# Sorted expert rows packed to 256 columns, scattered without router weights, and weighted by VectorE after a plain gather

## The chip, the core and the metric

The kernel runs on one core of a Trainium2 chip. Its engines are TensorE (PE, matrix products), VectorE (DVE), ScalarE (ACT), GpSimd (POOL) and SyncE (SP), each with its own queue of instructions, in order; 16 DMA engines move data between HBM and the on-chip memory. Engines wait for each other by semaphores. The metric is the device time of one execution in microseconds; lower is better.

## The reference

Everything is float32. The input x has 4 batches of 512 tokens and 256 columns, 16 tiles of 128 tokens in all.

```python
def ffn(x):                          # E = 16 experts, F = 96, top K = 2
    probs = softmax(x @ router_w)
    w, idx = top_k(probs, 2);  w = w / sum(w)
    h = silu(x @ gate_w[e]) * (x @ up_w[e])
    return sum over the token's two experts of w * (h @ down_w[e])

def attention(x):                    # 16 heads of 128, 4 key/value heads, rotary, causal
    ...

x = x + 0.5 * ffn(layernorm(x))
x = x + attention(layernorm(x))
x = x + 0.5 * ffn(layernorm(x))      # same weights as the first
```

## The kernel before

**Pools.** Each of the two ffn passes sends its 16 token tiles to the experts in two pools, four in all: pool 0 is the first pass's batch 0 (4 token tiles), pool 1 its batches 1 to 3 (12), pool 2 the second pass's batches 0 to 2 (12), pool 3 its batch 3 (4). A pool's pairs of token and expert are sorted by expert into tiles of 128 rows; each expert's rows start on a tile border, so pools 0 and 3 have 23 tiles and pools 1 and 2 have 39, with rows that no token fills. 124 tiles in all.

**Routing.** After the layer norm TensorE makes the router's logits. VectorE then runs `route` in seven parts (the largest, one-hot, the second largest, one-hot), TensorE sums ranks, and VectorE makes the places: `places` (L1144 and on), parts 0 to 3: tiles of each expert (L1151 to L1153), their running sum (L1155, L1156), the place of each expert and token (L1157), for each of the two choices a product and a sum (L1164, L1166), the cast to integers `pos` (L1168), and the table `tab` of each tile's expert (L1169 to L1171). `shares` (L1177, L1178) makes the router weights of the two choices: it writes the first into the last column of the tokens' rows and the second into `wgt`. Pool 0's places come ahead of pool 1's choices. The statistics and step helpers wait for their predecessor's write by `stat_step`.

**Scatter.** `scatter` on GpSimd writes each token tile's 128 rows of 257 columns by an indirect DMA into the sorted buffer `xs` in HBM, at the places of the first choice (L1504). Three steps later, when that DMA has landed (`first_in`), it copies the second weight into the last column (L1509) and writes the rows again at the places of the second choice (L1511). The buffers are first filled with zeros by SyncE in 8 DMAs (`zero_tiles`, L746), ahead of the expert weights (L726, L732). `xs` has 23 x 128 and 39 x 128 rows.

**Experts.** SyncE loads a tile of sorted rows from a fixed place (`load_tile`, L754) into a ring of ten and stores each tile's result into `ys` (`store_tile`, L759). Per tile: TensorE transposes (L1647), reads the expert's number from `tab` (L1641), makes gate and up (L1593); ScalarE silu (L869); VectorE the product h (L1189); TensorE transposes h (L1659) and makes down (L1593); VectorE evacuates it times the weight in the tile's last column (`evacuate`, L1195). In every second tile or so VectorE also splits attention weights (L1185). Other work stands at steps beside the tiles i of a pool: in pool 1 the attention norm of batch 0 (`first_norm`), in pool 2 the routing of pool 3 (`last_pool`).

**Gather.** The first pass gathers with an accumulating indirect DMA: rows of `ys` are added into x in the on-chip memory (L1529), first choices first; pool 0's eight gathers run beside pool 1's tiles, and the 24 of pool 1 are spread over attention groups by `GATHERS` (batch and group: the gathers in it). The second pass gathers plainly into a ring of 16 (L1524), and VectorE adds (L1281).

**Attention** runs batch by batch in groups of a key/value head, each engine by a table written out by hand (`ORDER`, `turn_of`); `spread` puts further steps between a group's items from one share of it to another. The last batch's tables also hold the choices and places of pool 2 (`third`, with `SHARES`), and its scatters. GpSimd does the rotary embedding (L1538, L1541, L1549), VectorE the maxima (L1374) and the sum of the heads' projections into x (L1401).

## Time and profile before

| | us |
|---|---|
| median of three runs | 955.19 |
| the runs | 954.72, 955.19, 957.50 |
| the profiled execution | 958.23 |
| its span in the profile | 956.3 |
| TensorE busy in it | 814.0 (85%) |
| VectorE busy | 641.9 (67%) |
| ScalarE busy | 573.4 (60%) |
| GpSimd busy | 449.6 (47%) |

The span is the time from the profile's first to its last instruction; all starts below are counted from its beginning. The profile has one execution, and its mean granted TensorE clock is 0.957 of full speed. In its order of time: preparation to about 50 us, the first pass's tiles to about 175, attention to 812, in whose last batch pool 2 is routed, and the second pass's tiles and gathers to 956. Issuing a DMA isn't counted as busy time, an indirect DMA on GpSimd is.

### The profile page before, as it was taken

The numbers are of one execution on the slowest core, as the hardware profiler recorded it, in microseconds if no ns is written. First come the engines' busy times: TensorE is split into PE (matmuls) and PEld (weight loads), VectorE is DVE, ScalarE is ACT, GpSimd is POOL, SyncE is SP. The second block draws the span as 40 slices with busy tenths as digits, with TensorE's granted clock in tenths as the row PEclk, the third lists the DMA queues.
The fourth block names the chain that finished last, engine by engine and source line by source line (L and its number), as shares of the span: only waits on it lengthen the run. The fifth ranks groups of instructions, "written<-read, shape, count | busy, mean of one in ns | idle before, by whom it ended". The sixth has DMA issues, their size and how long they took to land.

```text
span 956.3 us, 16375 instructions
## 1 busy us (share of the span) xinstructions
PE 814.0 (85%) x4840; PEld 686.8 (72%) x4840; DVE 641.9 (67%) x1519; ACT 573.4 (60%) x1536; POOL 449.6 (47%) x410
## 2 busy tenths in 40 slices
PE   4457989898999999999999999999987938989490
PEld 3446878677878788787888887787776737778370
DVE  6403665467887778787877887868789735654163
ACT  3124765676677777776877876886755624445140
POOL 1472142387485756753644653643435560030623
PEclk9977999999999999999999999999999988999785
DMA  9975994211001101000000000000000452366544
GB/s 346 343 219 168 266 248 122 78 23 23 6 12 18 23 1 22 13 1 1 2 1 1 1 2 1 2 1 6 2 1 1 177 154 63 106 199 178 154 150 153
DMA packets 53812, 78.60 MB, mean 82 GB/s; under 512 B 7648, under 2 KB 44512, under 8 KB 52576
## 3 DMA queue, kind: packets, MB, share of 16 engines
q1 hardware_dynamic: 41632, 55.50, 18.1%
q0 software_dynamic: 9216, 16.82, 7.2%
q10 hardware_dynamic: 2880, 5.24, 1.9%
q8 instruction: 42, 0.69, 0.3%
q14 instruction: 42, 0.34, 0.1%
HBM read 42.61 MB, written 34.93 MB: 81 GB/s over the span
## 4 chain that ended last, share of the span: by engine, by line
PE 50%; issue 17%; POOL 13%; DVE 8%; ACT 4%; DMA 3%; SPq 3%; another core or an unknown queue 2%; ACTq 0%; DVEq 0%; POOLq 0%
PE ps L1593 41%; PE ps L1787 4%; POOL sb_x L1529 3%; POOL sb_ropeB L1538 3%; POOL sb_xf L1541 3%; PE ps L1647 2%; POOL sb_wF L1549 1%; DMA sb_x<-ys,sb_pos 1%; POOL xs L1511 1%; PE ps L1659 1%; DVE sb_x L1401 1%; DVE sb_wF L1381 1%; DVE sb_nmax L1374 1%; POOL xs L1504 1%
## 5 line engine op out<-in xcount | busy, mean ns | idle before, releaser
L1593 PE MATMUL ps<-sb_wF 128*128 128x512 f32 (+2 forms) x1056 | 280.0, 387 | 21.6 <-DVE sb_wF L1381 8.9
L1593 PEld LDWEIGHTS ps<-sb_wF 128*128 128x128 f32 x1056 | 170.6, 192 | 35.9 <-DVE sb_wF L1381 11.9
L1538 POOL TENSOR_TENSOR sb_ropeB<-sb_ropeB,sb_sin 128x512 f32<-128x512 f32 x80 | 109.0, 1362 | 146.0 <-ACT sb_ropeB L941 146.0
L961 ACT ACTIVATE sb_prob<-ps,sb_nmax 128x128 f32<-128x128 f32 (+3 forms) x256 | 134.5, 527 | 59.1 <-DVE sb_nmax L1374 57.1
L1593 PE MATMUL ps<-sb_wF,sb_wA 128*128 128x512 f32 x576 | 156.6, 407 | 7.6 <-ACT sb_ropeB L941 6.3
L1374 DVE TENSOR_REDUCE sb_nmax<-ps 128x1 f32<-128x128 f32 (+3 forms) x256 | 122.3, 485 | 49.8 <-PE ps L1593 45.3
L1401 DVE SCALAR_TENSOR_TENSOR sb_x<-ps,sb_rinv,sb_x 128x256 f32<-128x256 f32 x256 | 122.7, 479 | 27.4 <-PE ps L1593 11.6
L1549 POOL TENSOR_TENSOR sb_wF<-sb_xf,sb_wF 128x384 fp32r<-128x384 f32 (+1 forms) x75 | 85.5, 1141 | 114.6 <-ACT sb_wF L953 114.6
L1381 DVE TENSOR_TENSOR sb_wF<-ps,sb_wF 128x512 fp32r<-128x512 f32 x160 | 109.5, 684 | 35.0 <-ACT sb_wF L970 32.3
L1593 PE MATMUL ps<-sb_wA,sb_wF 128*128 128x256 f32 x768 | 117.5, 290 | 12.8 <-DVE sb_x L1401 8.7
L970 ACT ACTIVATE sb_wF<-ps 128x512 fp32r<-128x512 f32 x160 | 95.6, 598 | 50.0 <-PE ps L1787 37.9
L1593 PEld LDWEIGHTS ps<-sb_wA,sb_wF 128*128 128x128 f32 x768 | 108.4, 193 | 23.4 <-issue 15.6
L1593 PEld LDWEIGHTS ps<-sb_wF,sb_wA 128*128 128x128 f32 x576 | 104.0, 192 | 28.7 <-ACT sb_ropeB L941 7.8
L1593 PE MATMUL ps<-sb_wF_raw,sb_hT 96*128 x248 | 85.1, 426 | 42.1 <-issue 21.8
L1541 POOL TENSOR_TENSOR sb_xf<-sb_xf,sb_ropeB 128x512 f32<-128x512 f32 x80 | 104.2, 1303 | 6.3
L1787 PE MATMUL ps<-sb_ident,sb_prob 128*128 128x128 f32 x640 | 96.9, 274 | 4.0 <-DVE sb_LC L1157 2.0
L1189 DVE TENSOR_TENSOR sb_sg<-sb_sg,ps 128x96 f32<-128x96 f32 x124 | 31.3, 252 | 87.7 <-ACT sb_sg L869 58.9
L1787 PEld LDWEIGHTS ps<-sb_ident,sb_prob 128*128 128x128 f32 x640 | 75.8, 141 | 15.6 <-issue 5.1
L940 ACT ACTIVATE sb_ropeB<-ps 64x512 f32<-64x512 f32 x80 | 47.7, 596 | 55.1 <-DVE sb_xf L1358 53.2
L1593 PEld LDWEIGHTS ps<-sb_wF_raw,sb_hT 96*128 96x128 f32 x248 | 38.6, 196 | 52.8 <-issue 50.2
L1529 POOL DMA_INDIRECT sb_x<-ys,sb_pos x32 | 51.2, 1600 | 52.9 <-DMA ys<-sb_wA_raw 47.1
L869 ACT ACTIVATE sb_sg<-ps 128x96 f32<-128x96 f32 x124 | 30.8, 249 | 69.2 <-PE ps L1593 57.1
(176 smaller groups left out, 1336.3 us busy)
## 6 DMA issues: line engine op xcount, KB each, us to landing
ys<-sb_wA_raw SPq DMA_DIRECT2D x124, 128.0 KB
xs<-sb_wA_raw SPq DMA_DIRECT2D x6, 1024.0 KB, 11.2
sb_wF_raw<-xs SPq DMA_DIRECT2D x44, 128.5 KB
sb_wA_raw<-xs SPq DMA_DIRECT2D x44, 128.5 KB
sb_work<-xs SPq DMA_DIRECT2D x36, 128.5 KB
sb_wA_raw<-in_wattn ACTq DMA_DIRECT2D x18, 256.0 KB, 3.9
sb_wF_raw<-in_wgu SPq DMA_DIRECT2D x4, 768.0 KB
sb_wF_raw<-in_wdn SPq DMA_DIRECT2D x4, 768.0 KB
```

Of the source, the lines that this page charges most:

```text
L940: nc.scalar.activation(ropeB[0:HP, slot], ps[HP:P, bank], ACT.Copy, scale=scale)
L961: nc.scalar.activation(prob[k % 2][:, h, 0:(i + 1) * P], ps[:, bank_of((k * G + h) % (UB * G)), 0:(i + 1) * P], ACT.Exp, bias=nmax[:, k % ...
L970: nc.scalar.activation(pT_at(tb, 0), ps[:, TBANK + tb % 2], ACT.Copy).then_inc(pt_hi, 1)
L1374: nc.vector.tensor_reduce(nmax[:, k % 2, h:h + 1], ps[:, bank_of((k * G + h) % (UB * G)), 0:(i + 1) * P], AX_X, ALU.max, negate=True).then ...
L1381: nc.vector.tensor_tensor(pT_at(tb, 1), ps[:, TBANK + tb % 2], pT_at(tb, 0).bitcast(F32), ALU.subtract).then_inc(pt_lo, 1)
L1401: nc.vector.scalar_tensor_tensor(x[:, b, i], ps[:, wo_bank(b, k, h // 2), at:at + D], rinv[:, k % 4, h:h + 1], x[:, b, i], ALU.mult, ALU.a ...
L1529: nc.gpsimd.indirect_dma_start(out=x[:, t // T, t % T], out_offset=None, in_=ys[q.p][:], in_offset=where, compute_op=ALU.add).then_inc(acc ...
L1538: nc.gpsimd.tensor_tensor(ropeB[:, slot], ropeB[:, slot], sin[:], ALU.mult).then_inc(rope_mul, 1)
L1541: nc.gpsimd.tensor_tensor(xf[:, slot], xf[:, slot], ropeB[:, slot], ALU.add).then_inc(rope_sum, 1)
L1549: nc.gpsimd.tensor_tensor(lo[:, part], xf[:, rope_slot(col), part], hi[:, part].bitcast(F32), ALU.subtract)\
L1593: return nc.tensor.matmul(out, lhsT, rhs, start=start, stop=stop)
L1787: ins = nc.tensor.transpose(ps[:, TBANK + tb % 2, h * P:(h + 1) * P], prob[k % 2][:, h, j * P:(j + 1) * P], ident[:])
```

## The change

Rows of 256 columns, with no weight in them. `xs` holds the sorted rows of a pool packed, an expert's rows right behind those of the one before, and 128 rows behind them; only those 128 are zeroed, by one DMA for each of the two buffers. Both choices are scattered from the same rows, all first ones and then all second ones, 8 (pools 0 and 3) or 24 (1 and 2) indirect DMAs with nothing between them, as soon as `places` part 2 has cast the packed places (`to`).

A tile still has 128 rows and belongs to one expert; it now begins at a row that a table `begin` holds, and may run over into the next expert's rows. SyncE reads the row's number for every load. `places` has five parts: 0 to 2 as said, 3 makes `tab` and `begin` in 13 small operations, 4 turns the packed places into those in `ys` (`pos`), which keeps its layout. `shares` comes last and writes both weights to `wgt`. The evacuation is a copy.

The first pass's gathers are plain, into a ring of four, and VectorE adds each result times its weight (`result`); the second pass's sums take the weight too. The steps beside the tiles, in the attention groups and in the last batch move to make room; the choices of pool 1 are made in two halves, of 8 and of 4 token tiles, behind pool 0's places.

```diff
-    xs = [nc.dram_tensor(f"xs{n}", (pools[n].ns * P, RW), F32) for n in range(2)]
+    xs = [nc.dram_tensor(f"xs{n}", (pools[n].pairs + P, D), F32) for n in range(2)]
...
-    LN_FIRST = {5: (0,), 6: (1,), 7: (2, 3), 9: (5, 6), 10: (7,)}
+    LN_FIRST = {6: (0,), 7: (1, 2), 8: (3,), 9: (5, 6), 10: (7,)}
...
-    GATHERS = {(0, 1): range(12, 16), (0, 2): range(16, 20), (0, 3): range(20, 26), (1, 1): range(26, 32)}
+    GATHERS = {(0, 1): range(12, 16), (0, 3): range(16, 20), (0, 4): range(20, 24), (1, 3): range(24, 28),
+               (1, 4): range(28, 32)}
+    RESULTS_AT = {1: (0.0, 0.3, 0.3, 0.5), 3: (0.25, 0.6, 0.6, 1.0), 4: (0.0, 0.4, 0.4, 0.9)}
...
-                2: [(0.02, 0.4, range(18, 25)), (0.7, 0.85, range(26, 28))]},
-        "pool": {3: [(0.0, 0.0, range(12 + SECOND))]},
+                2: [(0.02, 0.4, range(18, 25)), (0.7, 0.95, range(26, 30))]},
+        "pool": {3: [(0.0, 0.0, range(2 * MT))]},
...
+        return (row(pools[0], j % AR) if j < 2 * T else work[:, (j % AR) * D:(j % AR + 1) * D])
...
+        def zero_rows(n):
+            end = pools[n].pairs
+            sp.dma_start(xs[n][end:end + P, :], zeros()).then_inc(zero_out[n], 16)
         def load_tile(q, s):
             at = q.tiles + s
             if s == 0:
-                sp.wait_ge(scattered[q.p], 16 * q.nt)
+                sp.wait_ge(begin_done, q.p + 1)
+            first = nc.values_load(begin[s:s + 1, q.p:q.p + 1], engines=[mybir.EngineType.SP], min_val=0, max_val=q.pairs,
+                                   skip_runtime_bounds_check_because="the table holds the least of that and a place")
+            if s == 0:
+                sp.wait_ge(scattered[q.p], 16 * 2 * q.nt)
+                if q.n == 0:
+                    sp.wait_ge(zero_out[q.p], 16)
             if at >= XR:
                 sp.wait_ge(y_evac, at - XR + 1)
-            sp.dma_start(tile_at(q, at), xs[q.p][s * P:(s + 1) * P, :]).then_inc(xg_in[at % XR], 16)
+            sp.dma_start(tile_at(q, at), xs[q.p][bass.ds(first, P), :]).then_inc(xg_in[at % XR], 16)
...
+            te, end, base, scratch, count, first, back = (r["ex"][:, i] for i in range(7))
             place = r["L"][:, 0:q.nt * E]
             if part == 0:
                 dve.wait_ge(rank_done, q.p + 1)
-                link(nc.vector.tensor_scalar(r["exi"][:, 0], counts_at(q), float(P - 1), None, ALU.add))
-                link(nc.vector.tensor_scalar(r["exi"][:, 1], r["exi"][:, 0], 7, None, ALU.logical_shift_right))
-                link(nc.vector.tensor_copy(te, r["exi"][:, 1]))
+                link(nc.vector.tensor_copy(count, counts_at(q)))
+                link(nc.vector.tensor_tensor_scan(end, count, count, 0.0, ALU.add, ALU.max))
+                link(nc.vector.tensor_tensor(first, end, count, ALU.subtract))
             elif part == 1:
-                link(nc.vector.tensor_tensor_scan(end, te, te, 0.0, ALU.add, ALU.max))
-                link(nc.vector.tensor_tensor(base, end, te, ALU.subtract))
                 nc.vector.scalar_tensor_tensor(
                     place.rearrange("p (e t) -> p e t", e=E),
-                    base.rearrange("p (e o) -> p e o", o=1).broadcast_to([P, E, q.nt]), float(P),
+                    first.rearrange("p (e o) -> p e o", o=1).broadcast_to([P, E, q.nt]), 1.0,
                     ranks_at(q).rearrange("p (e t) -> p e t", e=E), ALU.mult, ALU.add).then_inc(rank_read, 1)
...
+                nc.vector.tensor_copy(r["to"][:, :, at:at + q.nt], r["pf"][:, :, 0:q.nt]).then_inc(to_done, 1)
+            elif part == 3:
+                link(nc.vector.tensor_scalar(r["exi"][:, 0], count, float(P - 1), None, ALU.add))
+                link(nc.vector.tensor_scalar(r["exi"][:, 1], r["exi"][:, 0], 7, None, ALU.logical_shift_right))
+                link(nc.vector.tensor_copy(te, r["exi"][:, 1]))
+                link(nc.vector.tensor_tensor_scan(end, te, te, 0.0, ALU.add, ALU.max))
+                link(nc.vector.tensor_tensor(base, end, te, ALU.subtract))
+                link(nc.vector.tensor_scalar(scratch, end, slot_index(q), None, ALU.is_le))
+                link(nc.vector.tensor_reduce(r["cnt"][:, 0:1], scratch, AX_X, ALU.add))
+                nc.vector.tensor_scalar(tab[:, q.p:q.p + 1], r["cnt"][:, 0:1], float(E - 1), None, ALU.min)\
+                  .then_inc(tab_done, 1)
+                link(nc.vector.scalar_tensor_tensor(back, base, -float(P), first, ALU.mult, ALU.add))
+                link(nc.vector.scalar_tensor_tensor(scratch, base, slot_index(q), back, ALU.is_le, ALU.mult))
+                link(nc.vector.tensor_reduce(r["cnt"][:, 1:2], scratch, AX_X, ALU.min))
+                link(nc.vector.scalar_tensor_tensor(r["cnt"][:, 1:2], slot_index(q), float(P), r["cnt"][:, 1:2], ALU.mult,
+                                                    ALU.add))
+                nc.vector.tensor_scalar(begin[:, q.p:q.p + 1], r["cnt"][:, 1:2], float(q.pairs), None, ALU.min)\
+                  .then_inc(begin_done, 1)
             else:
+                for k in range(2):
+                    moved = per_token(q, "lm", 2)
+                    link(nc.vector.tensor_tensor(plane(q, 1), plane(q, 2 + k),
+                                                 back.rearrange("p (o e) -> p o e", o=1).broadcast_to([P, q.nt, E]),
+                                                 ALU.mult))
+                    link(nc.vector.tensor_reduce(moved, plane(q, 1), AX_X, ALU.add))
+                    link(nc.vector.tensor_tensor(r["pf"][:, k, 0:q.nt], r["pf"][:, k, 0:q.nt], moved, ALU.subtract))
                 nc.vector.tensor_copy(pos[:, :, q.t0:q.t0 + q.nt], r["pf"][:, :, 0:q.nt]).then_inc(pos_done, 1)
-                link(nc.vector.tensor_scalar(r["ex"][:, 3], end, slot_index(q), None, ALU.is_le))
-                link(nc.vector.tensor_reduce(r["cnt"][:], r["ex"][:, 3], AX_X, ALU.add))
-                nc.vector.tensor_scalar(tab[:, q.p:q.p + 1], r["cnt"][:], float(E - 1), None, ALU.min).then_inc(tab_done, 1)
         def shares(q):
             dve.wait_ge(gtanh_done, q.p + 1)
-            tanh = gap(q, 1)
-            step(nc.vector.tensor_scalar(row_weights(q), tanh, 0.25, 0.25, ALU.mult, ALU.add))
-            nc.vector.tensor_scalar(wgt[:, q.t0:q.t0 + q.nt], tanh, -0.25, 0.25, ALU.mult, ALU.add)\
-              .then_inc(weight_done, 1)
-            settle()
+            for k, half in enumerate((0.25, -0.25)):
+                link(nc.vector.tensor_scalar(wgt[:, k, q.t0:q.t0 + q.nt], gap(q, 1), half, 0.25, ALU.mult, ALU.add))
+        def weighted_add(t, k, y):
+            return nc.vector.scalar_tensor_tensor(x[:, t // T, t % T], y, wgt[:, k, t:t + 1], x[:, t // T, t % T], ALU.mult,
+                                                  ALU.add)
+        def result(j):
+            t, k = pair(0, j)
+            dve.wait_ge(res_in[j % AR], 16 * (j // AR + 1))
+            if k == 1:
+                dve.wait_ge(res_done, j)
+            weighted_add(t, k, result_at(j)).then_inc(res_done, 1)
...
+            nc.vector.tensor_copy(yo(s), y_at(s)).then_inc(y_evac, 1)
...
-            if 12 <= i < 12 + T:
-                dve.wait_ge(acc_in[i - 12], accumulated(1))
-                norm_stats(stats, 0, i - 12, i - 12)
-            elif i == 16:
+            if 6 <= i < 6 + 2 * T:
+                result(i - 6)
+            if 14 <= i < 14 + T:
+                dve.wait_ge(res_done, T + i - 13)
+                norm_stats(stats, 0, i - 14, i - 14)
+            elif i == 18:
                 mean_start(stats, mv)
-            elif i == 17:
                 rsqrt_start(mv, rs)
-            elif i == 19:
+            elif i == 20:
                 rsqrt_step(rs)
-            elif i in (20, 21):
-                for t in range(2 * (i - 20), 2 * (i - 19)):
+            elif i in (21, 22):
...
-            elif i == 18:
+            elif 18 <= i < 23:
+                places(q, i - 18)
+            elif i == 23:
                 shares(q)
-                places(q, 0)
-            elif 19 <= i < 22:
-                places(q, i - 18)
...
+        def second_choices(first, last):
+            lcopy(pools[1], first // 2)
+            chosen[1] = (first, last)
+            for part in range(6):
+                route(pools[1], part)
+            del chosen[1]
+        lcopy(pools[0], 0)
+        for part in range(7):
+            if part == 3:
+                second_norm()
+            route(pools[0], part)
+        for part in range(5):
+            places(pools[0], part)
+        shares(pools[0])
+        second_choices(0, 2 * FIRST_HALVES)
+        second_choices(2 * FIRST_HALVES, pools[1].nt)
+        route(pools[1], 6)
+        for part in range(5):
+            places(pools[1], part)
+        shares(pools[1])
...
+            k, t = divmod(n, q.nt)
             if n == 0:
+                pool.wait_ge(to_done, q.p + 1)
+                if q.n == 1:
                     pool.wait_ge(xt_ps, NFIRST)
                 pool.wait_ge(xn_done[q.p], q.nt)
+            nc.gpsimd.indirect_dma_start(out=xs[q.p][:], out_offset=place_of(q, k, t), in_=row(q, t),
+                                         in_offset=None).then_inc(scattered[q.p], 16)
...
+            if j >= AR:
+                pool.wait_ge(res_done, j - AR + 1)
+            if j % (2 * T) == 0 and j >= 4 * T:
+                pool.wait_ge(proj_done, normed(j // (2 * T) - 1))
+            nc.gpsimd.indirect_dma_start(out=result_at(j), out_offset=None, in_=ys[q.p][:],
+                                         in_offset=where).then_inc(res_in[j % AR], 16)
```

Of `scatter` the diff shows the new lines only; the old ones stand in the kernel above.

VectorE at the start, from the places of pool 0 on. Before:

```order
L1177 TENSOR_SCALAR sb_wF_raw<-sb_lmO 128x4 [waits gtanh_done]
L1178 TENSOR_SCALAR sb_wgt<-sb_lmO 128x4
L1151 TENSOR_SCALAR sb_exiO<-ps 128x16 [waits rank_done,stat_step]
L1152 TENSOR_SCALAR sb_exiO<-sb_exiO 128x16 [waits stat_step]
L1153 CAST sb_exO<-sb_exiO 128x16 [waits stat_step]
L1155 SCALAR_TENSOR_TENSOR sb_exO<-sb_exO 128x16 [waits stat_step]
L1156 TENSOR_TENSOR sb_exO<-sb_exO 128x16 [waits stat_step]
L1157 SCALAR_TENSOR_TENSOR sb_LO<-sb_exO,ps 128x64 [waits stat_step]
L1164 TENSOR_TENSOR sb_lgO<-sb_lgO,sb_LO 128x64 [waits rank_read]
L1166 TENSOR_REDUCE sb_pfO<-sb_lgO 128x4 [waits stat_step]
```


After (two of the 13 small rows for `tab` and `begin` stand at its end; the rest of them, those for `pos` and the shares follow):

```order
L1163 COPY sb_exO<-ps 128x16 [waits rank_done]
L1164 SCALAR_TENSOR_TENSOR sb_exO<-sb_exO 128x16 [waits stat_step]
L1165 TENSOR_TENSOR sb_exO<-sb_exO 128x16 [waits stat_step]
L1167 SCALAR_TENSOR_TENSOR sb_LO<-sb_exO,ps 128x64 [waits stat_step]
L1174 TENSOR_TENSOR sb_lgO<-sb_lgO,sb_LO 128x64 [waits rank_read]
L1176 TENSOR_REDUCE sb_pfO<-sb_lgO 128x4 [waits stat_step]
L1174 TENSOR_TENSOR sb_lgO<-sb_lgO,sb_LO 128x64 [waits stat_step]
L1176 TENSOR_REDUCE sb_pfO<-sb_lgO 128x4 [waits stat_step]
L1178 CAST sb_toO<-sb_pfO 128x2x4 [waits stat_step]
L1180 TENSOR_SCALAR sb_exiO<-sb_exO 128x16
L1181 TENSOR_SCALAR sb_exiO<-sb_exiO 128x16 [waits stat_step]
```


Ahead of the cast that releases the scatters stand no shares and no tile counts any more, four small operations less; the tile counts and shares come behind it.

VectorE among the tiles of pool 1, where the norm of batch 0 begins. Before, with the statistics (L1040) of the first token tiles:

```order
L1040 BN_STATS sb_stats<-sb_x 128x6 [waits acc_in0]
L1189 TENSOR_TENSOR sb_sg<-sb_sg,ps 128x96 [waits silu_done]
L1195 TENSOR_SCALAR sb_wA_raw<-ps,sb_wF_raw 128x256 [waits y_out2,y_ps]
L1185 TENSOR_TENSOR sb_wA<-sb_wA_raw,sb_wA 128x512 [waits w_hi]
L1040 BN_STATS sb_stats<-sb_x 128x6 [waits acc_in1]
L1189 TENSOR_TENSOR sb_sg<-sb_sg,ps 128x96 [waits silu_done]
L1195 TENSOR_SCALAR sb_wA_raw<-ps,sb_wF_raw 128x256 [waits y_out3,y_ps]
L1040 BN_STATS sb_stats<-sb_x 128x6 [waits acc_in2]
```


After, some six tiles earlier, with the results (L1213; h is L1231, the evacuation L1237, the weights' split L1227):

```order
L1213 SCALAR_TENSOR_TENSOR sb_x<-sb_wF_raw,sb_wgt,sb_x 128x256 [waits res_in0]
L1231 TENSOR_TENSOR sb_sg<-sb_sg,ps 128x96 [waits silu_done]
L1237 COPY sb_wA_raw<-ps 128x256 [waits y_out4,y_ps]
L1227 TENSOR_TENSOR sb_wA<-sb_wA_raw,sb_wA 128x512 [waits w_hi]
L1213 SCALAR_TENSOR_TENSOR sb_x<-sb_wF_raw,sb_wgt,sb_x 128x256 [waits res_in1]
L1231 TENSOR_TENSOR sb_sg<-sb_sg,ps 128x96 [waits silu_done]
L1237 COPY sb_wA_raw<-ps 128x256 [waits y_out5,y_ps]
L1213 SCALAR_TENSOR_TENSOR sb_x<-sb_wF_raw,sb_wgt,sb_x 128x256 [waits res_in2]
```


A statistic that waited for an accumulated row has become a sum that waits for a gathered one.

SyncE from the last loads that fill the ring on. Before:

```order
L754 DMA sb_work<-xs 128x257 x3
L759 DMA ys<-sb_wA_raw 128x256 [waits y_evac]
L754 DMA sb_wF_raw<-xs 128x257 [waits y_evac]
L759 DMA ys<-sb_wA_raw 128x256 [waits y_evac]
L754 DMA sb_wF_raw<-xs 128x257 [waits y_evac]
```


After:

```order
L757 TENSOR_LOAD sb_begin
L765 ISA
L765 DMA sb_work<-xs 128x256
L770 DMA ys<-sb_wA_raw 128x256 [waits y_evac]
L757 TENSOR_LOAD sb_begin
L765 ISA [waits y_evac]
L765 DMA sb_wF_raw<-xs 128x256
```


Between a store and a load there is now a read of the register and an instruction for the address; the wait for `y_evac` stands behind the read.

## Rows read from the trace of the kernel before

**Rows 1.** us, busy us and count of each engine, TensorE clock, DMA share, GB/s, by window.

```profile
24.00:48.00 24.00, 10.93 (x54) 10.59 (x53) 11.72 (x42) 4.42 (x9) 10.91 (x14) 1.00 0.95 340
48.00:72.00 24.00, 13.30 (x50) 10.39 (x50) 2.24 (x7) 5.56 (x15) 18.74 (x26) 0.79 0.70 220
```

**Rows 2.** Chain of waits to 60 us: start, length, what.

```profile
26.05 20.84 issue
```

**Rows 3.** GpSimd's timeline, start: start, length, instruction, idle before and its releaser.

```profile
26.72 1.18 POOL L1504 DMA_INDIRECT xs<-sb_wF_raw,sb_pos  x1 [9.79 <-DVE sb_pos L1168]
...
38.68 0.98 POOL L1511 DMA_INDIRECT xs<-sb_wF_raw,sb_pos  x1 [0.28 <-POOL sb_wF_raw L1509]
45.73 0.96 POOL L1504 DMA_INDIRECT xs<-sb_wF_raw,sb_pos  x1 [6.08 <-issue]
47.00 0.96 POOL L1504 DMA_INDIRECT xs<-sb_wF_raw,sb_pos  x1 [0.30 <-issue]
...
77.07 0.98 POOL L1511 DMA_INDIRECT xs<-sb_wF_raw,sb_pos  x1 [0.28 <-issue]
```

**Rows 4.** VectorE's timeline at the start, same columns.

```profile
34.45 0.36 DVE L1097 COPY sb_LO<-ps 128x192 f32<-128x192 f32 x1 [8.08 <-issue]
...
42.98 0.49 DVE L1164 TENSOR_TENSOR sb_lgO<-sb_lgO,sb_LO 128x192 f32<-128x192 f32 x1
...
45.16 0.17 DVE L1170 TENSOR_REDUCE sb_cntO<-sb_exO 128x1 f32<-128x16 f32 x1
45.36 0.15 DVE L1171 TENSOR_SCALAR sb_tab<-sb_cntO 128x1 int32<-128x1 f32 x1
52.80 0.26 DVE L1189 TENSOR_TENSOR sb_sg<-sb_sg,ps 128x96 f32<-128x96 f32 x1 [7.29 <-ACT sb_sg L869]
```

**Rows 5.** TensorE's timeline, in the burst and among pool 1's tiles.

```profile
60.76 0.69 PE L1593 MATMUL ps<-sb_wF_raw,sb_hT 96*128 x2 [2.96 <-issue]
...
76.06 1.22 PE L1593 MATMUL ps<-sb_wF_raw,sb_hT 96*128 x2 [6.46 <-issue]
...
136.14 0.81 PE L1593 MATMUL ps<-sb_wF_raw,sb_xT 128*128 x4
...
137.62 0.81 PE L1593 MATMUL ps<-sb_wF_raw,sb_xT 128*128 x4
```

**Rows 6.** TensorE's reads of the expert's number: duration ns min/median/max, first and last start.

```profile
L1641 PEldq TENSOR_LOAD <-sb_tab x124: 296/308/795, 48.2 to 929.2; - x124
```

**Rows 7.** SyncE's timeline beside pool 1's tiles: a store and a load.

```profile
102.00 0.32 SPq L759 DMA_DIRECT2D ys<-sb_wA_raw  x1
102.36 0.43 SPq L754 DMA_DIRECT2D sb_wF_raw<-xs  x1
```

**Rows 8.** VectorE's timeline at the first attention norm's first statistics.

```profile
130.41 0.43 DVE L1040 BATCH_NORM_STATS2 sb_stats<-sb_x 128x6 f32<-128x256 f32 x1 [3.29 <-DMA sb_x<-ys,sb_pos]
...
130.91 0.48 DVE L1195 TENSOR_SCALAR sb_wA_raw<-ps,sb_wF_raw 128x256 f32<-128x256 f32 x1
```

**Rows 9.** TensorE's waits from 128 to 147: total, times, longest.

```profile
PE ps L1593 <- DVE sb_wA_raw L1195: 3.3, 2, 2.6
```

**Rows 10.** A gather of GpSimd in the timeline; below, the landing of all of L1529.

```profile
122.79 1.90 POOL L1529 DMA_INDIRECT sb_x<-ys,sb_pos  x1 [0.31 <-issue]
...
DMA to landing us min/median/max: 3.8/3.8/4.3
```

**Rows 11.** VectorE's waits from 224 to 264: total, times, longest.

```profile
DVE sb_stats L1040 <- DMA sb_x<-ys,sb_pos: 3.3, 1, 3.3
```

**Rows 12.** Windows of the last batch and of the last gathers, columns as rows 1.

```profile
740.00:760.00 20.00, 17.30 (x109) 14.40 (x110) 16.32 (x36) 12.93 (x33) 10.45 (x11) 1.00 0.48 173
890.00:900.00 10.00, 1.69 (x10) 1.32 (x10) 1.55 (x4) 1.18 (x4) 7.57 (x9) 0.90 0.54 160
```

**Rows 13.** GpSimd's scatters of pool 2: ns min/median/max, first and last start.

```profile
L1504 POOL DMA_INDIRECT xs<-sb_rowC,sb_pos x12: 956/960/1070, 752.3 to 779.4; - x12
...
L1511 POOL DMA_INDIRECT xs<-sb_rowC,sb_pos x12: 976/980/989, 759.1 to 785.4; - x12
```

142 lines of the change are left out of this document (57 added, 85 removed).

## The prediction

> **What bounds the kernel now.** I read the span in order of time. In its first 48 us the DMA engines are nearly full and TensorE works less than half of the time; what it needs, the first tile of sorted rows, comes late: the chain of waits stands in one piece of 20.84 us, to 46.88, for the rows that were scattered [rows 1, 2]. The scatters of pool 0 were issued by 39.66 (38.68 + 0.98), so they took 7.2 us to land among the zero fills and weights; those of pool 1 run from 45.73 to 78.05 (77.07 + 0.98) [rows 3]. During that burst TensorE gets little done although its operands are there: it stood still for 2.96 us with no cause shown until 60.76, the first such wait, and for 6.46 until 76.06 [rows 5], and from 48 to 72 was busy for 13.3 of 24 us, with 50 matrix products, at nine per tile, and a granted clock of 0.79 [rows 1]. It finishes some five tiles between 57.8 and 79, where the undisturbed pace is one per 1.48 us (136.14 to 137.62) [rows 5]. Beside the tiles of pool 1 the accumulating gathers are waited for once for long, 3.29 us at VectorE, 2.6 at TensorE behind it [rows 8, 9]; in attention once more, 3.3 us [rows 11]. Attention itself is bound by TensorE, except where pool 2 is routed: from 740 to 760 VectorE is busy for 16.3 of 20 us, its work packed between TensorE's [rows 12].
>
> **The start.** The zero fill shrinks from (23 + 39) tiles x 128 rows x 1,028 bytes, 8.2 MB, to two blocks of 0.13 MB; in a stretch that moves 340 GB/s [rows 1] that is 23 us of traffic. By itself it moves no issue of a scatter, since the first waits for VectorE's places, not for zeros [rows 3]; it lets them land sooner. Pool 0's scatters: ahead of them VectorE has four small operations less, at 0.20 each (45.16 to 45.36) [rows 4], so the first goes out near 26.0 instead of 26.72. Eight at 1.27 (0.96 and 0.30 between, with rounding; 45.73 to 47.00) [rows 3] end at 36.2; with two or three microseconds to land, tiles can be loaded from 39, 8 us earlier.
> That lead isn't all usable, because VectorE comes next. Pool 0's new parts of the places cost 13 small operations (2.6 us), 4 of 64 columns and 3 small (4 x 0.27 + 0.6 = 1.7; 64 columns aren't in the rows and lie between a small one's 0.20 and the 0.40 of 192, at 0.27 if a column costs the same) and the shares 0.4, 4.7 us, all inside the 8.08 us in which VectorE is idle before 34.45 [rows 4]: no cost; with that cover gone they would cost 4.7. Two thirds of pool 1's choices fit behind them. What is left after 34.45 is a third of the width: 12 steps of 64 columns, 12 x 0.27 = 3.2 instead of 12 at 0.40 (0.36 and the small ones' gap of 0.04; 4.8), and four small ones less (0.8), so that pool 1's rows are placed about 2.0 us earlier: its burst starts near 43.75 (I take 2.0 of the 2.4). It holds 24 scatters at 1.27, 30.5 us, instead of 32.3, and ends near 74.2 instead of 78.05: -3.8. But after placing, VectorE has 13 small operations (2.5), 2 x (0.49 + 0.40 + 0.20) + 0.2 = 2.4 [rows 4], a tenth less in overlaps, and 0.4 of shares, and is free near 48.1: the first h is at 48.2 instead of 52.80 [rows 4], 4.6 us earlier. From the burst's start to the first late release today are 12 us (45.73 to 57.8, where the wait of 2.96 begins); so the undisturbed stretch holds 2 us less at its end and 4.6 more at its beginning, a tile and a third more, 1.3 x 1.48 = 2.0. The burst's disturbed stretch is 1.8 us shorter, which at five tiles in 22 us is 0.4 tile, +0.6, rounded to +0.8. **Start: -3.8 - 2.0 + 0.8 = -5.0.** Bounds: -1 if the lead is lost again in the burst and its end moves by half, -12 if all 8 us of the lead count and the burst is milder.
>
> **Beside pool 1's tiles.** Accumulating gathers of 1.5 to 1.9 us [rows 10] become plain ones at the scatters' 0.96 [rows 3], and VectorE adds each result, at the 0.48 of the evacuation in the same stretch [rows 8]. The removed waits at TensorE are 2.6 us there and 0.7 at the next such place, 3.3 in all [rows 9]. What is late next: results have a ring of 4. The accumulating gathers landed in 3.8 us at the median of its row [rows 10], but the gather that ended the wait of 3.29 was issued 7.6 us earlier, in full DMA traffic (122.79 to 130.41) [rows 8, 10]. At 6.5, between the two, the first result is waited for 1.7 us and the fifth 1.1, of which VectorE's slack of 0.7 each (3.29 less 2.6) hides half: +1.4. The normalisation is one tile later and its transposes aren't, +1.5. **-0.4** (bounds -3.3 if landing takes under 5 us and all is hidden, +3 at 7.6).
>
> **Attention of the first batches.** 24 more gathers become cheaper for GpSimd by 0.6 each, and leave the late half of a group. The wait of 3.3 us at VectorE [rows 11] goes; 24 results at 0.48 come onto VectorE, which has idle time in those groups but is on the path in places: 24 x 0.1 = 2.4, less the 0.6 of a crowded group that becomes empty. **-1.5** (bounds -5 and +2; for the lower one the late weight steps too stop costing).
>
> **Pool 2's routing, in the last batch.** The places grow by 13 small operations (2.6) and 4 of 192 columns and 3 small (2.4), and the shares move behind the cast, 5 us of VectorE in the stretch where it is at 16.3 of 20 [rows 12]: about 4 on the path. Against it stand 24 scatters without the copy between, 34.1 (752.3 to 785.4 + 0.98) [rows 13] to 30.5 us; TensorE stands for a good two thirds of such a stretch, judging by five tiles in 22 us of the first: -2.4 of the 3.6. **+1.6** (bounds -3, the burst alone, and +5, all of VectorE's).
>
> **Pool 3's routing, beside tiles.** Two steps hold 2.6 and 1.7 us in slots whose tile takes 1.48, of which the tile's own two operations fill 0.65 (0.25 and 0.40, from the spacing of the rows) and leave 0.8: (2.6 - 0.8) + (1.7 - 0.8) = 2.7, less some lead of VectorE: **+2.2** (bounds 0, since its scatters go one tile earlier and are shorter, and +3).
>
> **At nothing.** The evacuation as a copy instead of a product with the weight; the tail's weighted sums, which landings release. SyncE gains a register read and an address instruction for each tile. Its work per tile today is a store of 0.32 and a load of 0.43 [rows 7]. The trace has no such read on SyncE; the nearest is TensorE's of the expert's number, 296 to 795 ns, median 308 [rows 6]. 0.32 + 0.31 + 0.05 + 0.43 + 0.1 of gaps = 1.2 of 1.48: hidden. Bounds: nothing at 0.58 or less, and the price of the second rival at 0.795.
> The Trainium skill, DMA: Bandwidth & Descriptors, section Latency and other measured facts, gives a floor of about 600 ns for such a load. TensorE's row, at half of it, disagrees. By the page SyncE would need 1.50 us per tile, 2.5 us more over the 124 tiles, and the sum would be -0.6 instead of -3.1.
>
> **The sum.** -5.0 - 0.4 - 1.5 + 1.6 + 2.2 = -3.1. Against the profiled execution: span 956.3 to 953.2, its own time 958.2 to 955.1. That execution stands 3.0 above the median of the three runs, 955.2, and the difference should carry over: **952.1 us**. A measurement of this kernel can tell 0.3%, 2.9 us, from no change.
>
> **Rivals.**
> *The gain is given back (0.20).* The start is bound by VectorE's longer preparation, the burst disturbs as long as before, and only -2 of the -5.0 is left; the rest stands: -0.1, or 955. For it: VectorE is free 9 us after the first tile could be loaded. Against it: the burst's end moves by itself, by counts of instructions. It is also the case in which the change doesn't do what it says: zero filling and the wait between the choices weren't on the path.
> *SyncE becomes the bound (0.08), slower.* If its read takes 0.795 [rows 6], a tile costs 1.70 us: 0.22 x 124 = 27 us, less what the ring of ten tiles and the disturbed stretches absorb (6 tiles ahead in each half, 17 us): +10 to +27, with the rest 962 to 979. It decides from 0.58 us on. Against it: the median of 308.
> *VectorE and the ring of four are the bound (0.14), slower.* Landings of 7.6 us in full traffic cost +3 beside the tiles, the same again in attention, where the gather waits in GpSimd's queue ahead of the ropes that TensorE needs, and all of pool 2's 5 us lie on the path. These are the upper bounds of three terms: -3.1 + 3.4 + 3.5 + 3.4 = +7.2, or 962 (959 to 965). For it: the wait that ended after 7.6 us. It decides from landings of about 6.5 us.
> *The bursts stop disturbing (0.13), much faster.* TensorE's late releases may hang on the scattered rows of 1,028 bytes that start nowhere even, or on the waits between them. Then of the 22 us for five tiles 12 to 14 come back, and 8 before 790: 925 to 938. Against it: plain gathers of 1,024 bytes, back to back, end in late releases too (from 890 to 900, while 17 of them run, TensorE is busy for 1.7 of 10 us [rows 12]).
> The Trainium skill, DMA: Bandwidth & Descriptors, section How a descriptor splits into AXI transactions, speaks for this rival: a transfer that doesn't start on a 256-byte border costs a further transaction, so 1,028 bytes at an odd place take six where 1,024 at an even one take four. That alone would leave the sum as it is, since GpSimd's issue sets the pace; no row shows whether it bears on the releases.
>
> **How the numbers follow.** The forecast's own case has 0.45 and reaches from 947 to 957. Its centre lies almost on the bound of 2.9: 0.25 of it is faster, 0.18 within, 0.02 slower. The first rival: 0.03, 0.15, 0.02. The two slower rivals: 0.22 slower. The fast one: 0.13 faster. Sum: faster 0.41, within 0.33, slower 0.26. The range has to leave out two in ten: the fast rival and the upper half of the slow ones, so 942 to 962.
>
> **What the changed profile would show.** First h near 48, GpSimd's long burst from 43.8 to 74.2 with 1.27 between scatters, and the steady pace of 1.48 reached about 5 us earlier than before. A read on SyncE of about 0.3 us. No wait over 2 us of VectorE for a result beside the tiles. The attention group that began near 224 takes about 4 us less than before; the last batch is longer around 740 to 752, and its burst is 3.6 us shorter. Wrong would be: first tiles that wait for SyncE, VectorE standing for landings four by four, or a burst during which TensorE keeps its pace.

## The result, and the profile after

| | before | after |
|---|---|---|
| median, us | 954.96 | 970.16 |
| all runs | 954.23 to 957.50 | 965.53 to 973.65 |
| profiled execution | 958.23 | 970.94 |
| its span | 956.3 | 969.1 |

The ratio is 1.0162, with a 95% interval of 1.0132 to 1.0192: the change made the kernel 15 us slower. The forecast was 952.1, the range ended at 962.

The table follows the lead or lag of the changed kernel through the span. The rows are starts of h, VectorE's product for each tile (L1189 before, L1231 after), and of GpSimd's first rotary product in attention's first and last group, all read from the timelines.

| | before | after | difference |
|---|---|---|---|
| h of tile 0 | 52.80 | 49.81 | -3.0 |
| tile 3 | 63.18 | 54.95 | -8.2 |
| tile 5 | 79.47 | 79.12 | -0.4 |
| tile 29 | 117.33 | 115.61 | -1.7 |
| tile 60 | 180.08 | 180.38 | +0.3 |
| last group of attention | 716.82 | 713.09 | -3.7 |
| tile 63 (pool 2's second) | 815.23 | 823.34 | +8.1 |
| tile 83 | 848.92 | 856.28 | +7.4 |
| tile 90 | 862.82 | 875.76 | +12.9 |
| tile 107 | 888.42 | 899.85 | +11.4 |
| tile 123 (the last) | 932.09 | 944.75 | +12.7 |
| end | 956.3 | 969.1 | +12.8 |

Lead is lost in four places: between tiles 3 and 5, 29 and 60, in the last group, and between 83 and 90. Three of the four are bursts of scatters. GpSimd's timeline shows the bursts as they were forecast, 1.26 or 1.27 us apart without a gap (it answers [rows 3]):

```profile
25.61 1.18 POOL L1553 DMA_INDIRECT xs<-sb_wF_raw,sb_toO  x1 [8.48 <-DVE sb_toO L1178]
...
34.71 0.96 POOL L1553 DMA_INDIRECT xs<-sb_wF_raw,sb_toO  x1 [0.30 <-issue]
45.05 0.96 POOL L1553 DMA_INDIRECT xs<-sb_wF_raw,sb_toO  x1 [9.38 <-DVE sb_toO L1178]
46.31 0.96 POOL L1553 DMA_INDIRECT xs<-sb_wF_raw,sb_toO  x1 [0.30 <-issue]
...
74.13 0.96 POOL L1553 DMA_INDIRECT xs<-sb_wF_raw,sb_toO  x1 [0.30 <-issue]
```

The windows (columns as in [rows 1]) show what TensorE does meanwhile. From 48 to 72 it is busy for 8.2 us, and was for 13.3; from 760 to 780 for 7.9 us, and the row of the kernel before for the same stretch stands below it:

```profile
48.00:72.00 24.00, 8.23 (x34) 6.81 (x34) 4.03 (x16) 2.73 (x9) 18.21 (x20) 0.78 0.49 160
760.00:780.00 20.00, 7.85 (x30) 5.88 (x29) 2.89 (x6) 1.69 (x5) 15.26 (x16) 0.62 0.34 124
```

```profile
760.00:780.00 20.00, 14.31 (x80) 11.16 (x79) 8.67 (x16) 6.32 (x15) 15.59 (x23) 0.91 0.62 189
```

All engines' timeline inside the first burst, after, shows what is late (start, length, instruction, and in brackets the idle time before and its releaser):

```profile
55.37 0.81 PE L1638 MATMUL ps<-sb_wF_raw,sb_xT 128*128 x4
...
56.02 0.38 PE L1692 MATMUL ps<-sb_ident,sb_wF_raw 128*128 128x128 f32 x2
...
60.35 0.69 PE L1638 MATMUL ps<-sb_wF_raw,sb_hT 96*128 x2 [3.95 <-issue]
...
60.88 0.27 PE L1706 MATMUL ps<-sb_ident,sb_sg 128*96 128x128 f32 x1
...
66.23 0.25 ACT L880 ACTIVATE sb_sg<-ps 128x96 f32<-128x96 f32 x1 [6.03 <-remote]
66.52 0.25 DVE L1231 TENSOR_TENSOR sb_sg<-sb_sg,ps 128x96 f32<-128x96 f32 x1 [8.26 <-issue]
...
68.33 0.38 ACT L876 ACTIVATE sb_xT<-ps 128x256 f32<-128x256 f32 x1 [1.84 <-remote]
...
71.13 0.42 DVE L1237 COPY sb_wA_raw<-ps 128x256 f32<-128x256 f32 x1 [4.36 <-remote]
...
73.23 0.27 ACT L886 ACTIVATE sb_hT<-ps 96x128 f32<-96x128 f32 x1 [4.52 <-issue]
...
73.66 1.21 PE L1638 MATMUL ps<-sb_wF_raw,sb_hT 96*128 x2 [11.35 <-issue]
```

TensorE's gate and up product of tile 4 (the fifth) ends at 56.2, and ScalarE's silu, which needs only that, starts at 66.23, after 6.03 us of standing whose releaser the profile can't name. In the same way the transposes that end at 56.4 are copied at 68.33, the down product that ends at 61.0 at 71.13, and the transposed h of 61.2 at 73.23. VectorE follows ScalarE after 0.3 us, and TensorE (73.66) follows ScalarE (73.23) after 0.4. So what comes from ScalarE or VectorE is passed on in a few tenths; what comes from TensorE is taken up 10 to 12 us behind its end here, of which the taking engine itself stands 1.8 to 6.0 us each time and is kept by its queue for the rest, and each tile hands over four times. I call this holding up. The profile doesn't show where in the chip it arises.

### The profile page after: what moved, and what is told of

It reads as the page before. It is cut to its first block, busy times and chain, and to the rows that moved or that the text cites. A ratio compares the mean times of both kernels' runs of the same rounds, so it can differ in the third digit from the quotient of the medians.

```text
span 969.1 us, 16829 instructions
## 1 busy us (share of the span) xinstructions
PE 817.1 (84%) x4840; PEld 689.7 (71%) x4840; DVE 665.5 (69%) x1624; ACT 573.1 (59%) x1536; POOL 424.3 (44%) x378
## 4 chain that ended last, share of the span: by engine, by line
PE 59%; DVE 12%; issue 12%; another core or an unknown queue 5%; ACT 4%; POOL 4%; DMA 2%; SPq 1%; POOLq 0%; DVEq 0%; ACTq 0%
PE ps L1638 48%; PE ps L1834 5%; PE ps L1692 2%; DVE sb_x L1441 2%; DVE sb_wF L1421 1%; POOL sb_xf L1586 1%; PE ps L1706 1%; DVE sb_nmax L1414 1%; POOL sb_ropeB L1583 1%; DMA sb_wF_raw<-ys,sb_pos 1%; ACT sb_prob L972 1%; PE ps L1655 1%; DVE sb_x L1213 1%; DVE sb_wF L1431 1%
## 5 line engine op out<-in xcount | busy, mean ns | idle before, releaser
L1638 PE MATMUL ps<-sb_wF 128*128 128x512 f32 (+2 forms) x1056 | 284.1, 390 | 26.9 <-issue 13.0
L1583 POOL TENSOR_TENSOR sb_ropeB<-sb_ropeB,sb_sin 128x512 f32<-128x512 f32 x80 | 103.8, 1297 | 150.8 <-ACT sb_ropeB L952 150.5
L1594 POOL TENSOR_TENSOR sb_wF<-sb_xf,sb_wF 128x384 fp32r<-128x384 f32 (+1 forms) x75 | 80.6, 1074 | 122.0 <-ACT sb_wF L964 121.7
L1638 PE MATMUL ps<-sb_wF_raw,sb_hT 96*128 x248 | 82.6, 416 | 48.8 <-issue 30.7
L1231 DVE TENSOR_TENSOR sb_sg<-sb_sg,ps 128x96 f32<-128x96 f32 x124 | 31.2, 252 | 88.4 <-ACT sb_sg L880 71.7
L1638 PEld LDWEIGHTS ps<-sb_wF_raw,sb_hT 96*128 96x128 f32 x248 | 39.7, 201 | 56.8 <-issue 56.4
L1237 DVE COPY sb_wA_raw<-ps 128x256 f32<-128x256 f32 x124 | 52.5, 423 | 39.5 <-remote 20.3
```

The source lines that it names most:

```text
L1237: nc.vector.tensor_copy(yo(s), y_at(s)).then_inc(y_evac, 1)
L1583: nc.gpsimd.tensor_tensor(ropeB[:, slot], ropeB[:, slot], sin[:], ALU.mult).then_inc(rope_mul, 1)
L1594: nc.gpsimd.tensor_tensor(lo[:, part], xf[:, rope_slot(col), part], hi[:, part].bitcast(F32), ALU.subtract)\
L1638: return nc.tensor.matmul(out, lhsT, rhs, start=start, stop=stop)
```

## The experiments

Kernels named a_ are made from the changed kernel, b_ from the kernel before. They fell on five chips, and **there are two kinds of chip**: on two of them the kernel before took 952.6 to 953.3 us, much as in the first comparison (954.96); on three it took 898.1 to 899.4. The two of the first kind came up twice each, at different times, and took as long both times; the three others came up once each, so that a difference of the moment isn't excluded for them. Each result below says which kind it was, "held" (953) or "free" (898), and is compared with the kernel before on its own chip. Which kind a kernel falls on isn't chosen; some are therefore there twice.

**Pool 2's burst: taken away, and spaced.** The edits, in the changed kernel: no scatters of pool 2 (a_p2none; the result isn't the reference's, since pool 2's tiles read pool 1's rows), the same in the kernel before (b_p2none), and a copy of one column with its wait ahead of each of pool 2's scatters, once (a_p2gap1) or three times (a_p2gap3):

```diff
+            if n and q.p == 2:
+                for _ in range(1):                      # 3 in a_p2gap3
+                    paused[0] += 1
+                    nc.gpsimd.tensor_copy(pause[:, 1:2], pause[:, 0:1]).then_inc(pause_set, 1)
+                    pool.wait_ge(pause_set, paused[0])
             nc.gpsimd.indirect_dma_start(out=xs[q.p][:], out_offset=place_of(q, k, t), in_=row(q, t),
```

> The changed kernel without the 24 scatters of pool 2 (its tiles read the rows that pool 1 left in the same buffer, so the result is not the reference's). Theory A, the burst of back-to-back scatters is what holds TensorE up between 752 and 813: the rest of attention then takes its busy time, some 42 us, and the whole kernel is 20 us or more shorter than the changed one, near 945. Theory B, the loss of 11 us after 747 is VectorE's longer places and the shares: then it stays, and the kernel is shorter by the few microseconds in which tiles wait for rows, near 965.

> The kernel before without the scatters (and weight copies) of pool 2, its result likewise not the reference's. Theory A: it gains too, but less than the changed kernel does, since its burst disturbed less (11 us less): near 942, within 3 us of the changed kernel without them. Theory B: it gains 0 to 5 us, to 950 or more, and stays 11 us ahead of the changed one.

> The changed kernel with one copy of a column and the wait for it between two scatters of pool 2, as between second choices before: 1.45 us from one to the next instead of 1.27. Theory A1, the rate of issue decides how late TensorE's neighbours are released: the loss after 747 falls from 11 to about 3 us, the kernel to some 962. Theory A2, it is the number or the bytes of scatters, whatever their rate: the burst lasts 4 us longer and the kernel is at 970 to 974.

> The same with three such copies, about 2.4 us from scatter to scatter, so that the 24 take 57 us instead of 30. Theory A1: the disturbance disappears, attention ends near 795, but the rows are there at 752 + 57 + 5 = 814 only, so that the tiles start about where they do before: 957 to 963. Theory A2: attention is disturbed over all of the 57 us, and the kernel is at 975 or more.

All four fell on a free chip (before: 898.06).

| kernel | us | ratio, interval |
|---|---|---|
| a_p2none | 896.41 | 0.9971 (0.9951 to 0.9991) |
| b_p2none | 896.87 | 0.9986 (0.9967 to 1.0004) |
| a_p2gap1 | 895.19 | 0.9965 (0.9950 to 0.9981) |
| a_p2gap3 | 907.17 | 1.0094 (1.0067 to 1.0121) |

None of the expectations was made for a chip on which the kernel before takes 898 us, and none of them is settled by these four. The profile of b_p2none shows where the time goes: with the same burst of pool 1 as in [rows 3], TensorE is busy for 23.5 of the 24 us in which it was busy for 13.3 [rows 1]:

```profile
48.00:72.00 24.00, 23.48 (x130) 20.60 (x131) 10.49 (x28) 14.91 (x47) 18.76 (x26) 1.00 1.01 325
```

Two things follow for the free kind. Pool 2's scatters cost nothing there (a_p2none is no faster than the changed kernel, below). And the two kernels without them differ in the last group, which I put down to VectorE's longer places: from the group's start to tile 63 it takes 79.2 us before (701.1 to 780.26) and 84.2 after (693.7 to 777.96), 5.0 us more. TensorE's waits of that stretch in the changed kernel (a_full), and below them the same wait in b_p2none, name the sum of the heads' projections into x, which VectorE makes in the same queue as the longer places:

```profile
PE ps L1638 <- DVE sb_x L1441: 5.9, 3, 4.4
```

```profile
PE ps L1596 <- DVE sb_x L1402: 1.4, 2, 1.3
```

**The whole changed kernel again.** a_full and a_full2 are the changed kernel, b_full is the kernel before; a_p2none2 and a_p2none3 repeat a_p2none, a_p2gap3b repeats a_p2gap3. a_late takes part 4 of pool 2's places and its shares, which only the gathers need, out of the last group:

```diff
-                2: [(0.02, 0.4, range(18, 25)), (0.7, 0.95, range(26, 30))]},
+                2: [(0.02, 0.4, range(18, 25)), (0.7, 0.95, range(26, 28))]},
...
+            elif i == 6:
+                places(pools[2], 4)
+            elif i == 7:
+                shares(pools[2])
```

> The changed kernel as it is, in a second comparison. The four kernels before ran on a chip on which the kernel before took 898 us instead of 955 and TensorE kept its pace through the bursts. Theory C, the 15 us of the first comparison exist only where bursts of scatters hold TensorE up: on a chip without that, the changed kernel is faster than the kernel before by what is left of the forecast's terms, 2 to 8 us, near 893; on a chip with it, it is 10 us or more slower, as in the first comparison. Theory D, the loss is of the program's own, in VectorE's steps and the ring of four: 5 us or more slower on either kind of chip.

> The changed kernel without the scatters of pool 2 once more (not the reference's result), beside the whole one. On a chip where bursts hold TensorE up, theory C gives 20 us or more less than the whole changed kernel; on one without, 0 to 4 us less. Theory D: 0 to 4 us less on either.

> The kernel before as it is, for a profile beside the changed kernel's on the same chip. On a chip where TensorE keeps its pace through the bursts (theory C): 895 to 900, 50 busy of 50 us between 50 and 100 but for the known waits, and no wait of ScalarE or VectorE over 2 us without a cause in pool 2's scatters. On one where it doesn't: 955, with the waits of the first profile.

> The changed kernel a third time. Theory C: 2 to 6 us under the kernel before where bursts don't disturb, 10 or more above where they do. By stages, where they don't: first h 3.7 us earlier, tiles at 1.42 instead of 1.48 us, 9 us ahead at the last group of attention, and 4 to 5 of them lost again in pool 2's routing and 1 to 2 in pool 3's.

> The changed kernel with part 4 of pool 2's places and its shares taken out of the last group of attention and done beside tiles 6 and 7 of pool 2 (only the gathers need them). If VectorE's longer places are what costs 4 to 5 us there, this gives back 2 to 3 us of it: on an undisturbed chip 892 to 893, 6 to 7 us under the kernel before. If the loss there is the scatters' or the loads' (rival), nothing changes.

> The changed kernel without the 24 scatters of pool 2 (not the reference's result), meant for a chip like that of the first comparison (the kernel before near 955). Theory E, the scatters hold up what others wait for from TensorE: pool 2's second tile comes near 790 instead of 823, and the kernel takes 930 to 940. Theory F, that chip is slow there for another reason: 820 and 967 or more. On a chip of the other kind both say 896.

> Pool 2's scatters alone at 2.4 us, 57 us of them. On a chip with the disturbance, theory E1: TensorE keeps its pace, attention ends near 795, pool 2's tiles wait for the rows until 817, and the kernel takes 960 to 965. Theory E2: attention is held up over all of the 57 us, pool 2's second tile comes at 830 or later, 975 or more. On one without: 907, as measured.

| kernel | chip | us | before | ratio, interval |
|---|---|---|---|---|
| a_full | free | 895.16 | 899.44 | 0.9964 (0.9944 to 0.9983) |
| a_p2none2 | free | 896.53 | 899.44 | 0.9972 (0.9950 to 0.9993) |
| b_full | held | 953.99 | 953.29 | 1.0009 (0.9982 to 1.0035) |
| a_full2 | held | 969.39 | 953.29 | 1.0170 (1.0127 to 1.0212) |
| a_late | held | 966.49 | 953.29 | 1.0126 (1.0090 to 1.0161) |
| a_p2none3 | held | 942.46 | 952.78 | 0.9879 (0.9824 to 0.9933) |
| a_p2gap3b | held | 956.55 | 952.78 | 1.0031 (0.9997 to 1.0065) |

Theory C holds: the same change is 4.3 us faster on a free chip and 16 slower on a held one. Theory D falls, and so does F, although E's numbers were a little low (tile 63 at 794.4 for 790, 942.46 for 930 to 940); B holds for the 5.0 us above and no more. Taking pool 2's scatters away is worth 27 us on a held chip (969.39 to 942.46) and nothing on a free one. a_late was 2.9 us faster than a_full2 where 2 to 3 were expected, but the two intervals overlap; in the profiles the stretch from the last group to tile 63 fell from 110.4 to 106.2 us. a_p2gap3b is the first sign that distance counts (a_p2gap1, the single copy in pool 2 alone, wasn't run on a held chip). Its three copies put 1.95 us between scatters, not the 2.4 I expected (the copies don't wait for each other as long as I thought), and with a burst of 46 us instead of 30 the kernel is 13 us faster than a_full2, and faster than E1's 960 to 965. TensorE now waits there for a named cause, the rows that come late:

```profile
PE ps L1702 <- DMA sb_wA_raw<-xs: 10.3, 2, 10.0
```

**All scatters spaced.** a_gap1all has the copy and its wait ahead of every scatter of the changed kernel. b_gap1 and b_gap1b (the same kernel twice) have it ahead of each first-choice scatter of the kernel before, whose second choices already had it:

```diff
             if n < q.nt:
+                if n:
+                    paused[0] += 1
+                    nc.gpsimd.tensor_copy(pause[:, 1:2], pause[:, 0:1]).then_inc(pause_set, 1)
+                    pool.wait_ge(pause_set, paused[0])
                 nc.gpsimd.indirect_dma_start(out=xs[q.p][:], out_offset=place_of(q, 0, n), in_=rows_of(q)[:, n],
```

a_best and a_best2 (the same twice) are a_late with all scatters spaced, and the gathers of the second pass too.

> The changed kernel with one copy and the wait for it ahead of each scatter of every pool, so that scatters go out each 1.45 us, as the second choices did before, instead of 1.27. On a chip with the disturbance, theory E1 (the rate of issue decides how much is held up): the losses in the bursts of pools 1, 2 and 3 fall back to the kernel before's, and it takes 953 to 960. Theory E2 (only the length and the number count): the bursts are 4 us longer each, and it takes 970 to 980. On a chip without it: 895 to 898.

> The kernel before with one copy of a column and its wait ahead of each first-choice scatter too, so that no two scatters stand closer than 1.45 us (before, the two of a pair took 2.72 together). On a chip with the disturbance, theory E1 (spacing is what counts): it falls from 953 to 930 to 940, and the change itself, at equal spacing, is worth 2 to 5 us (932 was measured for it). Theory G, the spacing only helps the changed kernel, whose rows are packed and aligned: 953 or more. On one without: 898 to 902.

> The kernel before with all scatters 1.45 us apart, once more, meant for a chip with the disturbance. Theory E1 (spacing is what counts): 930 to 940 instead of 953. Theory G, the spacing only helps the changed kernel, whose rows are packed and aligned: 950 or more. On a chip without it: 900, as measured.

> The changed kernel with all scatters 1.45 us apart, the gathers of the second pass spaced in the same way, and pool 2's part 4 and shares beside its tiles. With the disturbance, theory E1: the 932 of the spaced scatters, less 3 to 4 for the moved parts, less 8 to 13 for the last gathers, in whose burst TensorE now stands for 15 us: 916 to 922. If gathers disturb by another mechanism than scatters: 928 to 930. On a chip without it: 891 to 894.

> The changed kernel with all scatters and the second pass's gathers spaced to 1.45 us and pool 2's part 4 and shares beside its tiles, meant for a chip with the disturbance. There the kernel before with spaced scatters took 926, the changed one with spaced scatters 932. If spacing helps gathers as it helps scatters (theory E1): less 8 to 13 in the last stage and 3 for the moved parts, 916 to 922. If the last gathers disturb in another way: 929 to 933. On a chip without the disturbance: 901, as measured.

| kernel | chip | us | before | ratio, interval |
|---|---|---|---|---|
| a_gap1all | held | 932.21 | 952.78 | 0.9769 (0.9724 to 0.9815) |
| b_gap1b | held | 926.45 | 952.72 | 0.9729 (0.9686 to 0.9772) |
| a_best2 | held | 919.92 | 952.56 | 0.9668 (0.9632 to 0.9705) |
| b_gap1 | free | 900.35 | 898.82 | 1.0014 (0.9992 to 1.0036) |
| a_best | free | 901.07 | 898.82 | 1.0012 (0.9994 to 1.0031) |

GpSimd's timeline of a_gap1all shows the spacing, 1.46 us (the copy and its wait stand between):

```profile
52.18 0.98 POOL L1561 DMA_INDIRECT xs<-sb_wF_raw,sb_toO  x1 [0.28 <-issue]
...
53.64 0.98 POOL L1561 DMA_INDIRECT xs<-sb_wF_raw,sb_toO  x1 [0.28 <-issue]
```

That is 0.19 us more than after the change, on a burst of 24, and the changed kernel went from 969 to 932 us. Theory E2 falls: the bursts are longer, and hold up less. The direction is E1's, its size isn't: it expected 953 to 960 for a_gap1all, the losses of the kernel before, and 930 to 940 for b_gap1b. So does theory G fall: b_gap1b keeps its rows of 1,028 bytes, and gains 26 us. Its windows from 48 to 72, against 13.3 of 24 us in [rows 1], and over pool 2's whole burst:

```profile
48.00:72.00 24.00, 18.49 (x96) 14.56 (x96) 6.41 (x18) 10.70 (x33) 19.20 (x35) 1.00 0.90 286
737.59:773.31 35.72, 29.86 (x195) 24.63 (x193) 24.81 (x52) 18.13 (x47) 28.13 (x47) 1.00 0.62 207
```

Pool 2's whole burst in the kernel before:

```profile
752.31:786.32 34.01, 22.24 (x134) 17.86 (x132) 16.43 (x33) 10.26 (x26) 25.71 (x36) 0.94 0.64 217
```

TensorE's busy share of pool 1's burst, on held chips, goes with the mean distance of its scatters: 0.38 after the change (1.26 us apart), 0.47 before (1.36), 0.68 and 0.72 in a_gap1all and b_gap1b (1.47). In pool 2's it is 0.57 (1.27), 0.65 (1.44, of single distances from 1.27 to 2.8), 0.83 and 0.84 (1.46 and 1.51). On a free chip a_full has 0.87 in pool 1's burst at 1.28. Spacing gives back about half of what a held chip costs and not all: 926 and 932 us stand against 898 for the kernel before on a free one. And each wider distance in these runs was made by a copy and its wait, so that the distance and the pause itself weren't told apart.

a_best2 gained as theory E1 had it, 919.92 for an expected 916 to 922: gathers hold up too, and spacing eases them (from tile 105 to the last it took 47.7 us in a_gap1all, 858.1 to 905.8, and 38.0 in a_best2, 852.1 to 890.1; a_best2 also has the moved parts and ran on the other held chip). Each remaining wait of TensorE without a named cause is 1.3 us at most in that stage:

```profile
PE ps L1656 <- issue: 9.3, 10, 1.3
```

On a free chip spacing costs: a_best missed its 891 to 894 and is 6 us behind a_full (901.07 to 895.16, on different free chips). By the profiles 3.7 us of it are there at tile 60 (161.87 to 158.13), where pool 1's rows come later, and 3.9 more stand behind tile 123, where the spaced gathers end later; between 60 and 160 TensorE now waits for loads of tiles:

```profile
PE ps L1710 <- DMA sb_wF_raw<-xs: 3.6, 2, 3.1
```

**Bytes or rows.** a_narrow (run twice) scatters only 64 of the 256 columns in pool 2, into a buffer of its own, 1.27 us apart as after the change (not the reference's result).

> The changed kernel with pool 2's 24 scatters of 64 columns instead of 256 into a buffer of their own (not the reference's result), still 1.27 us apart. With the disturbance, theory E1a, what counts is the bytes in flight: pool 2's second tile comes near 790, the kernel takes 940 to 945 as without the scatters. Theory E1b, what counts is the number of rows (descriptors) per time: 820 and 966 to 970. On a chip without it: 896.

> The changed kernel with pool 2's 24 scatters of 64 columns instead of 256 into a buffer of their own (not the reference's result), still 1.27 us apart, meant for a chip with the disturbance. Theory E1a, what counts is the bytes in flight: pool 2's second tile comes near 790, the kernel takes 940 to 945, as without the scatters. Theory E1b, what counts is the number of rows per time: 820 and 966 to 970. On a chip without it: 895, as measured.

On a free chip it took 895.25 (ratio 0.9963, 0.9945 to 0.9982), on a held one 967.21 (before: 952.56; 1.0177, 1.0122 to 1.0233), as the changed kernel. With a quarter of the bytes, tile 63 came at 820.6 (a_full2: 823.2; without the scatters: 794.4). The window shows TensorE busy for 7.6 of 20 us while the DMA engines are at 0.08:

```profile
760.00:780.00 20.00, 7.58 (x26) 5.75 (x25) 2.30 (x5) 1.27 (x3) 15.12 (x17) 0.66 0.08 26
```

So it isn't the bytes and not the load of the DMA engines. What is left is the number of rows, or of indirect DMAs, per time; these two weren't told apart.

## Why the prediction was wrong, step by step

**The step that failed** is one sentence on the start: "The burst's disturbed stretch is 1.8 us shorter, which at five tiles in 22 us is 0.4 tile". It took the rate at which a burst lets tiles through as given, and the burst's length as what changes. The rate itself was misread: between 57.8 and 79 the kernel before makes three tiles, not five (h at 58.84, 63.18 and 70.26, the next at 79.47); the 50 products of [rows 1] begin ten microseconds earlier, ahead of the first late release. And the rate is what changes. In pool 1's burst on held chips, a tile takes 2.2 to 2.5 us with scatters 1.47 apart (tiles 3 to 5: 56.05 to 60.48 in b_gap1b, 51.15 to 56.13 in a_gap1all; the pace stays so to tile 11), 8.1 with the kernel before's mix of distances and 12.1 after the change; a free chip needs 1.5 at 1.28 (a_full, tiles 3 to 11, 53.2 to 65.3). The length matters much less. The same step stood in the term for pool 2 ("TensorE stands for a good two thirds of such a stretch"; in that burst it stood for a third, 11.8 of 34.0 us, before, and for 0.43 of it after) and in that for pool 3. That the change makes the scatters denser stood in the working, as 24 x 1.27 instead of 32.3, and was counted as a gain only. That the denser scatters make the difference between the two kernels is inferred from the runs with wider distances; no run gave the kernel before the changed one's distances, or the other way round.

- **Start, -5.0.** The burst was as long as forecast and 0.9 to 1.3 us later: 45.05 to 75.09 (43.75 to 74.2 forecast). First h came at 49.81, not 48.2, with a lead of 3.0. In a_gap1all, on a held chip, it came at 48.09, and at 48.9 to 49.8 in the six profiles of the changed kernel and its variants on held chips whose first scatters weren't spaced, so that the first scatters seem to cost 0.8 to 1.7 us already. Tile 3 was 8.2 us ahead. Then two tiles in 24 us, and -0.4 was left. On a free chip it is 48.01 against 51.73 at tile 0 (a_full, b_p2none), -3.7, and -4.2 at tile 60.
- **Beside pool 1's tiles, -0.4:** +2.0 in the first comparison (tiles 29 to 60), inside its bounds; +0.6 for the pair b_full and a_full2. VectorE waited once, for the first result:

```profile
120.33 0.48 DVE L1213 SCALAR_TENSOR_TENSOR sb_x<-sb_wF_raw,sb_wgt,sb_x 128x256 f32<-128x256 f32 x1 [3.48 <-DMA sb_wF_raw<-ys,sb_pos]
```

The landing was quick (gather at 115.90, 4.4 us), but the first gather began 1.1 us later than before (114.83 there), since it waits for the last store of pool 0, and SyncE had fallen behind: that tile's evacuation was at 108.90, its store at 110.99; before, 0.5 us lay between (110.36 and 110.88). The transposes' wait of 1.4 for the normalisation is as forecast (1.5).
- **Evacuation, "at nothing".** Probably wrong, in the kernel's favour: the copy takes 0.42 us instead of 0.48, and the undisturbed pace is 1.42 us per tile instead of 1.48 (tiles 91 to 107: 22.7 us and 23.8). The two differences are equal, but the profile names no wait of TensorE in that stretch, in either kernel, so that the copy is the cause isn't shown.
- **SyncE, "hidden".** The read takes 0.27 us at the median, so the rival of 0.795 falls, and the floor of about 600 ns for such a load (the Trainium skill, DMA: Bandwidth & Descriptors, Latency and other measured facts) isn't borne out on SyncE either:

```profile
L757 SPq TENSOR_LOAD <-sb_begin x124: 3/273/458, 28.1 to 933.5; - x124
```

But working without a pause SyncE needs 1.29 us per tile (102.73 to 104.02), of 1.42, and so catches up slowly after each stop; I put the late store down to that.

```profile
102.73 0.43 SPq L770 DMA_DIRECT2D ys<-sb_wA_raw  x1
103.64 0.33 SPq L765 DMA_DIRECT2D sb_work<-xs  x1
104.02 0.80 SPq L770 DMA_DIRECT2D ys<-sb_wA_raw  x1
```

- **Attention, -1.5.** From tile 60 to the last group: -4.0 in the first comparison, -4.5 on a free chip, +0.6 for the pair b_full and a_full2. Inside its bounds, and not settled better than that.
- **Pool 2's routing, +1.6:** +11.8. Of its two parts, VectorE's was near (4 forecast, 5.0 measured without scatters), the burst's had the wrong sign: -2.4 forecast, about +6.8 measured as the rest, and about +10 for the pair b_full and a_full2, in which the whole is +15.0.
- **Pool 3's routing, +2.2.** +5.5 (tiles 83 to 90). On a free chip +1.9 (a_full against b_p2none), the forecast's own size; the rest I put down to its scatters, 1.27 apart, which no run changed by themselves. At equal spacing it is still +3.6 (a_gap1all against b_gap1b, tiles 81 to 90).

On a free chip the sum as a whole came out: -4.3 measured, -3.1 forecast. That is luck in part, since its terms don't all agree (a_full against b_p2none: attention -4.5 for -1.5, the last group +3.9 for +1.6). Of the rivals, the one with VectorE and the ring of four came nearest to the time (959 to 965 for 970), by another cause; the fast one, that the late releases hang on rows of 1,028 bytes at odd places, was the right question with the wrong lever: b_gap1b has those rows and is held up far less. The rule on transfers that don't start on a 256-byte border that stood behind it (the Trainium skill, DMA: Bandwidth & Descriptors, How a descriptor splits into AXI transactions) may be true, and no run here shows a part of it in this. The prediction's count from it was wrong: worked out from that rule, as an estimate, a row of 1,028 bytes takes five transactions wherever it starts (at a multiple of 4), not six, and one of 1,024 bytes on a border four.

At equal spacing, on held chips, the change itself is worth a loss of about 6 us (932.2 to 926.5, on two chips on which the kernel before takes 952.8 and 952.7); expected were a gain of 2 to 5. Up to the last group it is 5.5 us ahead (697.8 and 703.3), and the last group takes it back and 2 more (tile 63 at 789.3 and 787.2), where VectorE's longer places lie, and pool 3's follow. On free chips (a_full against b_p2none) the lead up to the last group is 8.7 us and the two stretches cost 3.9 and 1.9, for 7.6 and 3.6 here, so that equal spacing doesn't take away all that a held chip adds; what the rest is stays open.

## What to carry to other kernels

A loss that is read from one trace as "so many tiles in so many microseconds" is a rate under one set of conditions; before it is scaled, look whether the edit changes those conditions, here the distance between indirect DMAs. Work that a change puts on an engine should be laid where nobody waits for it: moving the parts of the places that only the gathers need from the last group to the tiles was worth 3 us, on the edge of the noise. And where two chips can differ, a comparison holds for its kind: the change is to be had on one (0.996), the spaced one on the other (0.967), and none of the versions tried is best on both.

## What the hardware showed that I had not expected

- Two kinds of chip, 953 and 898 us for the same kernel, with the same durations of single instructions (a scatter 0.96 us, h 0.25). The difference lies in stretches with dense indirect DMAs: on the held kind, what comes from TensorE is taken up to 12 us behind its end (61.2 to 73.23), with the taking engine standing for 1.8 to 6.0 us at a time.
- It sets in some microseconds behind the burst's first DMA: about 10 in pool 1's (45.05 to 55.2, the start of VectorE's first wait without a named cause), 4.5 in pool 2's (752.2 to 756.7, ScalarE's).
- 0.19 us of distance, made by a copy and its wait, are worth much: 1.27 us apart cost the changed kernel 37 us against 1.46 on a held chip (969.39 and 932.21).
- TensorE's granted clock is lower where TensorE stood: 0.78 from 48 to 72 and 0.62 from 760 to 780, where a_gap1all and b_gap1b have 1.00. In those mixed windows the engine runs at 1.2 GHz for part of the time, and a down product takes 1.21 us at 73.66, behind 11.35 us of standing, where it took 0.69 at 60.35. This adds to the loss; as its cause it doesn't fit, since a_full on a free chip has 0.87 from 48 to 72 and TensorE busy for 23.4 of the 24 us.
